# Attention stage: GpSimd's sends parted by its selections

## What is computed

```python
xn = _layernorm(x, axis=-1)
# attention: 16 heads of 8 features
q, k, v = split(einsum('bte,fe->btf', xn, in_proj_weight))
attention = softmax(einsum('bhtd,bhkd->bhtk', q / sqrt(8), k) + causal_mask)
attn = einsum('bhtk,bhkd->bhtd', attention, v) -> out_proj_weight
# experts: one shared, seven routed, the best two by softmax(x @ wr.T + rb), weights normed
expert(h) = (silu(h @ g.T) * (h @ u.T)) @ d.T      # 128 -> 352 -> 128
x = x + attn + shared(xn) + sum_e w[e] * expert_e(xn)
```

## Time and profile before

| | before |
|---|---|
| median of 3 runs | 509.91 us (509.83 to 512.62) |
| the profiled execution | 512.13 us, of which the span from first to last instruction is 510.1 us |
| mean granted TensorE clock of it | 0.935 |
| PE busy | 458.3 us (90%) |
| DVE, ACT, POOL busy | 350.2, 306.4, 296.1 us |
| selections (L635) | 128, 643 ns mean |
| sends of tokens (L613) | 64, 972 ns mean, from 129.5 to 294.4 us |
| sends of results (L663) | 76, 1043 ns mean |

### The profile page before, as it was taken

One profiled execution on the slowest core, in us unless ns is written; L12 is line 12 of the kernel. 1 busy time (PEld: TensorE's weight loads), 2 busy tenths in 40 slices (PEclk: granted clock), 3 DMA queues, 4 the chain that ended last, 5 costly groups with the idle time before them and its releaser, 6 DMA issues.

```text
span 510.1 us, 12198 instructions
## 1 busy us (share of the span) xinstructions
PE 458.3 (90%) x3919; PEld 328.0 (64%) x3923; DVE 350.2 (69%) x722; ACT 306.4 (60%) x661; POOL 296.1 (58%) x424
## 2 busy tenths in 40 slices
PE   8888998989878887878898999989899999979996
PEld 4766555646555554555565667868668788858874
DVE  6796998868766565665555048757667687656897
ACT  2756776757665565665555667646547676546653
POOL 1445997968767567667677540255364497856300
PEclk9999999979998699898756699999999999989999
DMA  9786999897753454355237024767767668730762
GB/s 249 234 256 216 317 317 308 289 377 252 249 158 110 124 147 153 96 159 152 89 106 273 22 86 141 228 207 226 242 210 247 223 195 279 246 119 28 227 196 72
DMA packets 60412, 99.80 MB, mean 196 GB/s; under 512 B 11045, under 2 KB 29226, under 8 KB 59328
## 3 DMA queue, kind: packets, MB, share of 16 engines
q1 hardware_dynamic: 55872, 90.57, 56.0%
q0 software_dynamic: 4480, 8.47, 4.9%
HBM read 60.85 MB, written 38.94 MB: 196 GB/s over the span
## 4 chain that ended last, share of the span: by engine, by line
PE 65%; ACT 8%; issue 5%; SPq 5%; another core or an unknown queue 5%; DVE 4%; DMA 2%; ACTq 0%; DVEq 0%; POOL 0%
PE ps L894 11%; PE ps L892 11%; PE ps L893 10%; PE ps L1042 6%; PE ps L975 6%; PE ps L983 5%; ACT sb_work L767 3%; PE ps L1046 3%; PE ps L1025 2%; PE ps L1210 2%; SPq L494 2%; PE ps L971 2%; PE ps L1027 2%; DMA sb_ring<-qk 2%
## 5 line engine op out<-in xcount | busy, mean ns | idle before, releaser
L1416 DVE TENSOR_REDUCE sb_blockmax<-ps 128x6 f32<-128x768 f32 x128 | 121.3, 955 | 67.2 <-PE ps L983 61.9
L767 ACT ACTIVATE sb_work<-ps 128x768 f32<-128x768 f32 x128 | 104.0, 813 | 79.2 <-PE ps L971 60.8
L663 POOL DMA_INDIRECT ys<-sb_v_all,sb_xn_all x76 | 79.3, 1043 | 76.0 <-DVE sb_v_all L1543 57.1
L635 POOL TENSOR_SCALAR_AFFINE_SELECT sb_work<-sb_work 128x512 f32<-128x512 f32 x128 | 82.2, 643 | 56.1 <-ACT sb_work L767 54.7
L893 PE MATMUL ps<-sb_ring,sb_wb 128*128 128x512 f32 (+5 forms) x231 | 83.2, 360 | 0.0
L975 PE MATMUL ps<-sb_ring 32*128 32x256 f32 x256 | 53.0, 406 | 29.4 <-ACT sb_work L767 23.2
L1521 DVE TENSOR_TENSOR sb_v_all<-ps,sb_v_all 128x512 f32<-128x512 f32 (+3 forms) x93 | 57.2, 615 | 25.7 <-ACT sb_v_all L839 10.4
L613 POOL DMA_INDIRECT xs<-sb_xn_all,sb_posu x64 | 62.2, 972 | 13.7 <-issue 13.7
L975 PEld LDWEIGHTS ps<-sb_ring 32*128 32x128 f32 x256 | 26.5, 196 | 60.3 <-issue 52.1
L983 PE MATMUL ps<-sb_mask_b,sb_ident_b 128*128 128x256 bf16 x256 | 55.1, 301 | 0.0
L839 ACT ACTIVATE sb_v_all<-ps 128x512 f32<-128x512 f32 (+3 forms) x93 | 49.5, 532 | 9.0 <-PE ps L894 5.4
(11 more groups left out here) (165 smaller groups left out, 1063.0 us busy)
## 6 DMA issues: line engine op xcount, KB each, us to landing
sb_wb<-wd SPq DMA_DIRECT2D x50, 384.0 KB
sb_ring<-qk SPq DMA_DIRECT2D x64, 256.0 KB
wd<-sb_wb SPq DMA_DIRECT2D x8, 1088.0 KB, 5.2
sb_wb<-wd SPq DMA_DIRECT2D x25, 320.0 KB
xs<-sb_o_all SPq DMA_DIRECT2D x19, 260.0 KB, 3.6
qk<-sb_ring SPq DMA_DIRECT2D x32, 128.0 KB
sb_work<-ys SPq DMA_DIRECT2D x16, 256.0 KB, 3.2
sb_xn_all<-xs SPq DMA_DIRECT2D x15, 260.0 KB
```

The costliest lines, as they stand in the source:

```text
L635: pool.affine_select(out=o, in_=o, compare_op=ALU.is_ge, fill=0.0, base=0, pattern=[[0, 4], [1, 128]], channel_multiplier=-1)\
L663: pool.indirect_dma_start(out=ys_d, out_offset=bass.IndirectOffsetOnAxis(ap=row, axis=0), in_=yst[i % NYS][:, EMB * j:EMB * j + EMB], in_o ...
L767: act.activation(part.rearrange("p (k h q) -> p h k q", h=2, q=128), ps[:, 4:6, 0:HEAD].rearrange("p h (k q) -> p h k q", q=128), ACT.Exp, ...
L1416: dve.tensor_reduce(blockmax[:, p % 2, q, a:b + 1, 0:3], ps[:, a:b + 1, 0:HEAD].rearrange("p h (k c) -> p h k c", c=128), AX.X, ALU.max).t ...
```

## The change

In each of its steps, GpSimd now keeps one send for the end of the step, and makes any other send of that step between its two selections. Even steps from 24 to 62 and the steps 31, 39, 47 and 55 have two sends, so there one stands between the selections and one behind them. Odd steps with one send, and step 23, are as they were. Which rows are sent, and in which order, stays the same, and no wait is added or taken away.

```diff
             for n in STEPS:
                 b, j = quad(n)
 
+                between = max(sent(n - 1), sent(n) - 1)
                 if isq(n):
                     for k in range(2):
                         pair = PAIRS[1 - k]
+                        if k:
+                            sends(sent(n - 1), between)
                         pool.wait_ge(s["ex"], 2 * n + k + 1)
...
                 if 0 <= n + 1 < MT * EXPERTS:
                     split_block((n + 1) // MT, (n + 1) % MT)
-                sends(sent(n - 1), sent(n))
+                sends(between, sent(n))
```

## The result

The changed kernel took 483.25 us (median of 4 runs, 482.12 to 488.42). Beside it the kernel before took 511.26 us (4 runs, 509.83 to 514.72). The ratio is 0.946, with a 95% interval of 0.938 to 0.955: faster by 28 us. The profiled executions are 482.78 and 512.13 us, 29.35 us apart.

A forecast was written before the change was run, and what follows sets the result against it. PE's results, held behind two GpSimd sends in a row, bound the attention; 14 x 6.40 + 4 x 7.15 = 118.2 us, 125.0 with the clock, gains 25.3 + 0.7 = 26 us: 484 us, range 475 to 499.

The forecast's parts named there:

- The hold: Attention, even steps: two GpSimd sends 1.27 us apart make PE's results late, costing 1.33 us a pair of steps.
- the stretch: Attention from the value sums of step 24 to those of step 60: 18 pairs, 150.32 us, forecast 125.0 us.
- The bound taken from the expert phase: Expert-phase sends 1.67 us apart leave PE fully busy, so the new order's 1.80 us should too.
- All of the 1.33 us: Attention pairs at full clock: parting the sends gains the whole 1.33 us, out of bounds 0 to 1.33 us.
- the partial rival: Half of the double sends still hold PE: gain 13 us, 497 us; chance 8%.
- The pair takes 6.35 + 0.05 = 6.40 us: Pair with three sends: 6.35 us as before the sends began, plus 0.05 us (0 to 0.10) for the late second selection.
- Pairs with four sends: Four attention pairs whose odd step also has two sends: GpSimd is slowest, 7.15 us each, no gain.
- The clock: Attention from step 24 to 60: time at 1.2 instead of 2.4 GHz falls from 32% to 20% (bounds 8% and 32%).
- the forecast's formula: Attention from step 24 to 60 takes 118.2 / (1 - 0.27 x) us, x being the share of time at 1.2 GHz.
- Outside the stretch: Steps 60 to 63 hold one more pair of sends: gain 0.7 us (0 to 1.5); the expert phase stays.
- The rival that the sends are not the cause: Something else in even steps delays PE; only the late selection remains, +1 to 2 us, 511 us; chance 7%.
- The rival that the hold moves and doubles: Any two sends within about 2 us delay PE, so each pair is delayed twice: 524 us; chance 5%.

The follow-up runs named there:

- the two memset kernels: Kernel before with a GpSimd memset between a step's two attention sends: one column 512.41 us, ratio 0.997; 512 columns 494.67 us, ratio 0.968 (chip A).
- the kernel with all sends between: Changed kernel with the single send of each odd step also between its two selections: 483.65 us, ratio 0.949 (chip A).
- the long memset: Kernel before with a 512-column memset between a step's two sends, which start 1.68 us apart: 494.67 us, ratio 0.968 (chip A).
- The repeat: Kernel before and changed kernel run once more, unaltered, together on chip C: 512.7 us and 485.03 us, the latter at ratio 0.947.
- the kernel with 256-column memsets: Kernel before with a 256-column memset between a step's two attention sends: 468.19 us, ratio 1.005 on chip B; 498.52 us, ratio 0.985 on chip D.

## Why the prediction was right, point by point

Forecast 484 us, measured 483.25; or, as a gain, 26 us forecast and 28 us measured, since the forecast started from the 509.91 us of three runs and the comparison has 511.26. The mechanism is the forecast one. That the number came out so close is in part luck: two terms of the sum were off by over 6 us each, in opposite directions.

- **The hold comes from the two sends in a row, and parting them lifts it.** Right: PE's idle behind the exponential is 3.9 us (forecast: under 5), and the stretch is 124.83 us (forecast: 125.0). Shown by the two memset kernels, of which one changed the neighbourhood and not the distance, and the other the distance and not the place between the selections, and by the single sends of the kernel with all sends between, which begin where the second send did and hold 0 to 0.3 us. The bound taken from the expert phase, 1.67 us apart and PE undisturbed, was the right row: 1.68 us is what the long memset gave.
- **All of the 1.33 us goes.** Nearly: 0.25 us of it stays (1.54 against 1.29 us), and only on chips with the hold. The forecast of 1.3 us was that much too low. This is the partial rival in small, spread over every pair rather than in half of them.
- **The pair takes 6.35 + 0.05 = 6.40 us.** Wrong in size: 6.77 us at the median. Of the 0.37 us, 0.26 are that rest of the hold (6.77 against 6.51 on the chip without it) and 0.11 GpSimd's list. In the list, the chain's piece from the exponential to the value sums was forecast as 4.33 us (144.07 to 148.40) and measured as 4.41. It is set by the exponential's end, so any rest of the hold ahead of it adds in full. Taking half of 0 to 0.10 us for "slack elsewhere" was the error: in the changed kernel GpSimd is the one that releases the value sums, and nearly no pair has slack.
- **Pairs with four sends take 7.15 us and gain nothing from the parting.** 7.37 us in the first comparison and 7.26 on the mean without the hold: four turns of 1.82 us are 7.28, where the forecast had rounded the gaps down to 7.15. That they gain nothing was wrong: left in a row they took 7.99 us, and the clock fell twice behind them; the stretch was 5.2 us longer in all.
- **The clock: 20% of the time at the lower level.** It was 0%: the granted clock was 1.00 in the whole stretch. At x = 0 the forecast's formula gives 118.2 us. It was 124.8 because the pairs are longer: 14 pairs of 6.81 on the mean and 4 of 7.37 are 124.8 us. The clock term was mis-sized by 6.8 us one way and the pair terms by 6.6 us the other way, and they cancelled: that is the luck in 484. The direction, that PE's denser work would hold the clock at least partly, was right; a stretch of 6.8 us at the lower level did come, but right behind the end of it.
- **Outside the stretch.** 0.7 us were forecast, 3.9 us measured: 1.6 us ahead of it and 1.8 us in the expert phase. The 1.6 us are from the clock ahead of the first send, as said above. The repeat has 1.4 us ahead of the stretch and 0.2 in the expert phase, so the 1.8 us are no effect of the change either. What can be put down to it in the two traces is some 26 us, the forecast's own number.
- **The rival that the sends are not the cause** fell, but on chip B its "the change gives nothing" would, by the estimate below, have been the right forecast. There the Trainium skill's rule in SBUF — State Buffer, "Who interferes with whom", agrees with the runs: PE waits for no send at 1.47 us (exponential after 1.30 us). On chip D it doesn't: the same sends, results 1.3 us late. No row of one profile could have told that the hold can be absent; the prediction and the first comparison hold where it is present.
- **The rival that the hold moves and doubles** fell for its size: at 1.8 us no full hold is seen. The 0.25 us that are left follow the place of a single send against the value sums, as the steps counted above show, and not the gap between two.

By sums of the traces, the changed kernel on the chip without the hold would take about 464 us: the 470.73 us of the kernel with memsets in the expert phase less the 6.9 us that they cost (205.86 against 198.99). That is an estimate, beside a before of 464.6: there the change would be worth nothing and cost nothing.

How the path runs from a send to a late semaphore of PE is open. The Trainium skill says in Perfetto Trace Analysis, "DMA Instruction — SWDGE (GPSIMD)", that such an instruction's end in the profile is the end of writing descriptors and not of moving data. In these traces the hold did outlast the second send's end by 0.7 us. That fits with something that goes on behind the instruction, but no run here separates the writing from the moving.

## What to carry to other kernels

Where a waiting engine starts late behind PE though PE's row says it was done, look at what GpSimd issues at that moment: indirect DMAs 1.3 us apart can hold PE's results by 1.35 us, and 1.7 us apart they hardly do. What then remains is smallest where a send begins some 0.3 us ahead of the matmuls in question and not right behind their start. Space them with work that GpSimd has to do anyway, since each 512-column filler took 0.71 us of GpSimd's list and gave part of the gain back. And time such a change on more than one chip: the same edit was worth 28 us in the first comparison, 26 us on chip C (510.77 against 485.03) and, by estimate, nothing on chip B.

## What was not expected of the hardware

- **One program took 9% less on one of four chips.** The kernel before took 511.98, 510.77 and 506.67 us on chips A, C and D and 464.6 us on B. Two places account for most of it: the attention stretch, 150 us against some 123 (in the kernel with 256-column memsets), and the expert phase, 214 against 199 us. Chip B was used once, so its state at that time can't be told from the chip.
- **The distance is judged sharply.** 1.27 us apart every double send held PE. At 1.47 us, all of twelve did up to step 48, and of five behind it one did, one did in part and three did not. At 1.68 us none did. That is at the full clock, in even steps.
- **A single send holds a little, by its place.** With a send that began 0.02 to 0.07 us behind an even step's value sums the exponential was 0.15 us and more late in every case, with one 0.31 to 0.36 us ahead of them at most 0.05 us; without the hold, on chip B, sends in either place left it at 1.29 us.
- **The clock came back whole.** With the holds the stretch's granted clock was 0.84, without them 1.00, and with four of them put back 0.96; the forecast had expected it to come back by half.
